# VectorE subtracts the outputs' low part from the PSUM bank in place of a second ScalarE copy and a GpSimd subtraction

## The reference, cut to what matters

```python
x = x + xattn(layernorm(x), ctx)     # out @ Wo + bo + lora(out, o_down, o_up)
x = x + ffn(layernorm(x))            # bit_linear, depthwise conv, silu, bit_linear
# in the attention, per head:
s = einsum(q, k) * SCALE;  p = softmax(s);  o = einsum(p, v)
```

## Time and profile before

| | |
|---|---|
| median of 3 runs | 1537.39 us (1535.62 to 1537.73) |
| profiled execution | 1535.5 us |
| its span in the trace | 1533.5 us |
| granted TensorE clock, mean | 0.983 of full |

### The profile page before, as it was taken

How to read it: one execution, slowest core, us unless ns; L and a number is a source line. 1 busy time by engine, 2 the same in 40 slices (tenths; PEclk the granted TensorE clock), 3 DMA queues, 4 the chain that set the end, 5 groups by cost and what they waited for, 6 DMA issues and landing times.

```text
span 1533.5 us, 33070 instructions
## 1 busy us (share of the span) xinstructions
PE 1409.5 (92%) x10604; PEld 1159.5 (76%) x10650; DVE 1195.5 (78%) x3059; ACT 1182.3 (77%) x3909; POOL 668.1 (44%) x1058
## 2 busy tenths in 40 slices
PE   7899999999999999999999999999999999999762
PEld 4688778787777878777787878788787777878541
DVE  4363698787969878796887878688787878788888
ACT  3477787978878797887879788787978788797832
POOL 2354444445444444544544454444445444444420
PEclk9999999999999999999999999999999999999985
DMA  9210100000010100000010000001000000100000
GB/s 279 53 31 16 31 16 28 20 28 30 24 34 15 33 11 28 30 28 29 15 44 1 29 28 28 29 15 44 8 23 28 28 29 15 44 1 1 29 15 14
DMA packets 41144, 47.13 MB, mean 31 GB/s; under 512 B 3024, under 2 KB 35216, under 8 KB 41104
## 3 DMA queue, kind: packets, MB, share of 16 engines
q1 hardware_dynamic: 41104, 46.62, 10.1%
HBM read 36.13 MB, written 10.49 MB: 30 GB/s over the span
## 4 chain that ended last, share of the span: by engine, by line
PE 43%; DVE 30%; ACT 17%; issue 9%; DMA 1%; DVEq 0%; POOL 0%; SPq 0%; POOLq 0%; ACTq 0%
PE PS L500 10%; ACT SM L751 8%; PE PS L462 6%; PE PS L443 5%; PE PS L513 5%; PE PS L478 4%; PE PS L487 4%; PE PS L452 3%; PE PS L591 2%; DVE HP L1003 2%; DVE GBS L1062 2%; DVE MX L914 2%; DVE GBS L1086 2%; DVE HP L1009 2%; ACT QM L719 2%
## 5 line engine op out<-in xcount | busy, mean ns | idle before, releaser
L1238 POOL TENSOR_TENSOR SM<-SM,RC 128x496 f32<-128x496 f32 (+1 forms) x512 | 324.2, 654 | 738.6 <-DVE RC L908 738.6
L751 ACT ACTIVATE SM<-PS,MX 128x124 f32<-128x124 f32 x1024 | 359.9, 367 | 159.1 <-DVE SM L916 155.8
L500 PE MATMUL PS<-KT,QM 128*128 128x128 f32 x2048 | 278.1, 279 | 24.0 <-ACT SM L751 24.0
L500 PEld LDWEIGHTS PS<-KT,QM 128*128 128x128 f32 x2048 | 249.4, 192 | 38.6 <-ACT SM L751 38.1
L751 ACT ACTIVATION_READ_ACCUMULATOR SM<-PS,MX 128x1 f32 x1024 | 212.2, 207 | 0.0
L1269 POOL TENSOR_TENSOR OTl<-OF,OTh 128x256 fp32r<-128x256 f32 x256 | 204.1, 797 | 10.4 <-ACT OF L745 10.4
L487 PE MATMUL PS<-IDF,SM 128*128 128x128 f32 x1024 | 168.4, 287 | 16.6 <-POOL SM L1238 16.5
L743 ACT ACTIVATE OTh<-PS 128x256 fp32r<-128x256 f32 x256 | 100.4, 392 | 93.5 <-PE PS L478 92.5
L914 DVE TENSOR_REDUCE MX<-PS 128x4 f32<-128x496 f32 x256 | 170.5, 666 | 0.4 <-issue 0.4
L478 PEld LDWEIGHTS PS<-PT,V 128*64 128x64 f32 x2048 | 106.6, 136 | 82.3 <-issue 75.4
L478 PE MATMUL PS<-PT,V 128*64 128x128 f32 x2048 | 168.6, 286 | 0.0
(11 more groups left out here) (166 smaller groups left out, 3511.5 us busy)
## 6 DMA issues: line engine op xcount, KB each, us to landing
XIN<-in_x SPq DMA_DIRECT2D x16, 512.0 KB, 3.5
XRES<-in_x SPq DMA_DIRECT2D x16, 512.0 KB, 4.6
out_y<-HP SPq DMA_DIRECT2D x15, 512.0 KB, 3.2
CRAW<-in_ctxT SPq DMA_DIRECT2D x16, 256.0 KB, 2.7
RRAW<-in_ctxT SPq DMA_DIRECT2D x32, 128.0 KB, 2.9
QM<-in_Wq SPq DMA_DIRECT2D x1, 1024.0 KB, 9.1
GBS<-in_Wo SPq DMA_DIRECT2D x1, 1024.0 KB, 14.0
k_ipa_columns<-HP SPq DMA_DIRECT2D x1, 1024.0 KB, 6.5
```

The lines of the kernel that those rows point to most:

```text
L500: m = mm(psS[:, h, :], QM[:, 2 * q + h // 2, h % 2, TOK * b:TOK * b + TOK], KT[:, 2 * q + h // 2, b, :], start=True, stop=True)
L751: m = act.activation(SM[s % 2][:, h, 0:ORG], psS[:, h, 0:ORG], ACT.Exp, bias=MX[s % 2][:, h:h + 1], accum_out=SU[s % 2][:, h:h + 1])
L1238: m = pool.tensor_tensor(part, part, RC[c % 2][:, 4 * i:4 * i + 4].unsqueeze(2).broadcast_to(shape), ALU.mult)
```

## The change

ScalarE copies the bank `psO` once, into `OTh`, and signals `ot_high` with that. VectorE gets a new function, `output_low`: it waits for `ot_high` and writes `OTl` = `psO` - `OTh`, reading the bank itself, and signals `ot_done`. It stands in VectorE's step behind `attend_sums` and V's copy and ahead of `attend_maxima`; in the drain it follows the order of `output_copies`. `p_v` waits for `ot_done` in place of `ot_high`, since VectorE now reads the bank after ScalarE. The tile `OF` and GpSimd's `attend_low` are gone.

```diff
@@ -186,7 +186,6 @@
         SM = [sb(f"SM{i}", [P, 4, TOK]) for i in range(2)]
         PT = sb("PT", [P, 4, TOK])
         OT = [[sb(f"OT{i}{c}", [P, 2, TOK], F32R) for c in range(2)] for i in "hl"]
-        OF = sb("OF", [P, 2, TOK])
         MX = [sb(f"MX{i}", [P, 8]) for i in range(2)]
         SU = [sb(f"SU{i}", [P, 8]) for i in range(2)]
         RC = [sb(f"RC{i}", [P, 8]) for i in range(2)]
@@ -467,7 +466,7 @@
                 if gc.exists():
                     q, b = divmod(c, NB)
                     pe.wait_ge(pt_done, gc.count(CHUNKS, c + 1))
-                    need(pe, ot_high, gc.count(CHUNKS, c))
+                    need(pe, ot_done, gc.count(CHUNKS, c))
                     if b == 0:
                         u = 2 + 6 * q
                         pe.wait_ge(unit_free[0], gc.count(UNITS // 2, (u + U_V[0]) // 2 + 1))
@@ -535,7 +534,7 @@
                         pe.wait_ge(unit_free[0], g.count(UNITS // 2, UNITS // 2))
                         pe.wait_ge(s_used, g.count(CHUNKS, CHUNKS))
                         pe.wait_ge(pt_done, g.count(CHUNKS, CHUNKS))
-                        pe.wait_ge(ot_high, g.count(CHUNKS, CHUNKS))
+                        pe.wait_ge(ot_done, g.count(CHUNKS, CHUNKS))
                         pe.wait_ge(fin_done, g.count(2, 0))
                     if j >= len(F1_BANKS):
                         pe.wait_ge(g_done, g.count(CT, j + 1 - len(F1_BANKS)))
@@ -740,9 +739,7 @@
                 gc, c = chunk_at(g, s - 3)
                 if gc.exists():
                     act.wait_ge(o_full, gc.count(CHUNKS, c + 1))
-                    act.activation(OT[0][c % 2][:], psO, ACT.Identity)
-                    need(act, ot_done, gc.count(CHUNKS, c))
-                    act.activation(OF[:], psO, ACT.Identity).then_inc(ot_high, 1)
+                    act.activation(OT[0][c % 2][:], psO, ACT.Identity).then_inc(ot_high, 1)
 
             def exponentials(g, s):
                 if g.exists():
@@ -906,6 +903,12 @@
                     dve.tensor_reduce(SU[c % 2][:, 4:8], SM[c % 2][:, :, ORG:TOK], AX.X, ALU.add).then_inc(sum_done, 1)
                     dve.wait_ge(sum_done, gc.count(CHUNKS, c + 1))
                     dve.reciprocal(RC[c % 2][:], SU[c % 2][:]).then_inc(rec_done, 1)
+
+            def output_low(g, s):
+                gc, c = chunk_at(g, s - 3)
+                if gc.exists():
+                    dve.wait_ge(ot_high, gc.count(CHUNKS, c + 1))
+                    dve.tensor_tensor(OT[1][c % 2][:], psO, OT[0][c % 2][:].bitcast(F32), ALU.subtract).then_inc(ot_done, 1)
 
             def attend_maxima(g, s):
                 if g.exists():
@@ -1181,6 +1184,10 @@
                     value_copy(g, n + HALVES)
                 if g.shift(1).exists(1):
                     value_copy(g.shift(1), n)
+                if is_drain(g) and n == 3:
+                    output_low(g, 2)
+                if n % 2 == 0 and not (is_drain(g) and n == 4):
+                    output_low(g, n // 2)
                 if n % 2 == 0:
                     attend_maxima(g, n // 2)
                 if g.reg is None and g.off == 0:
@@ -1261,14 +1268,6 @@
             for n in range(EARLY_HALVES, HALVES):
                 project(At(0), n)
 
-            def attend_low(g, n):
-                s, half = divmod(n, 2)
-                gc, c = chunk_at(g, s - 3)
-                if half == 1 and gc.exists():
-                    pool.wait_ge(ot_high, gc.count(CHUNKS, c + 1))
-                    pool.tensor_tensor(OT[1][c % 2][:], OF[:], OT[0][c % 2][:].bitcast(F32),
-                                       ALU.subtract).then_inc(ot_done, 1)
-
             def residual(g, n):
                 if n in (16, 18, 20, 22) and g.exists():
                     b = (n - 16) // 2
@@ -1286,7 +1285,6 @@
                     finish(g.shift(-1), n)
                 residual(g, n)
                 attend(g, n)
-                attend_low(g, n)
 
             run_groups(pool, steps)
```

## The result

The changed kernel takes **1543.0 us** in the median (1542.3 to 1544.5, six runs), the kernel before 1536.8 beside it (1535.5 to 1537.7): a ratio of 1.0043, interval 1.0030 to 1.0056. It is slower by 6.2 us, 0.4%. The direction was forecast, and the range held the time; the forecast itself, 13 us, was double.

What follows compares the result with a forecast made beforehand. No engine alone bounds the kernel; TensorE's few waits in 14 periodic groups decide. Terms 0.33 + 0.13 - 0.10 + 0.26 + 0.33 = +0.95 us a group, +13.3 in all, gave 1551 us (+0.9%), range 1536 to 1566.

Steps and rivals of the forecast that it cites:

- scores of step 7: TensorE's scores that wait for ScalarE's exponentials: VectorE's insertions in steps 4, 5 and 6 delay them by +0.33 us a group.
- lower bound: The forecast's faster end, 1546 us: each insertion taken at 0.34 less 0.08 us of overlap.
- Step 5: 0.33 - 0.33 = 0: VectorE in step 5: the insertion's 0.33 us is paid back by the tiny scale instruction no longer held by GpSimd's subtraction.
- a sign that the prediction had named as proving it wrong: Maxima of steps 6, 15 or 1 beginning no later than before; a group of 89 us or less was the alternative.
- steps 4 and 9: VectorE instructions held until GpSimd's normalisation ends (context's subtraction, convolution): the insertion fills that stall and costs 0.
- Step 7 itself: VectorE after V's copy in step 7: the subtraction makes the maxima start at 715.20 rather than 715.07, +0.13 us a group.
- the scores of step 2: They already wait on the exponentials of step 1, so that step's insertion costs its full +0.33 us a group.
- The scores of step 0: Insertions in steps 14 and 15 delay step 15's exponentials by 0.66 us; 0.40 of room leaves +0.26 a group.
- The scores of step 14: VectorE's delays in steps 10 and 11 against two copies fewer on ScalarE (-0.54): sum -0.10 us a group.
- Rival 1: No stall is filled: steps 4, 5 and 9 cost their 0.33 too, +1.0 us a group more, 1565 us; chance 0.17.
- Rival 3: VectorE's subtraction hides in waits for scores, ScalarE's release wins: -0.54 before step 14's scores, 1530 us; chance 0.12.
- Rival 2: GpSimd's freed port gives back more: step 10's gate also goes clear, +0.42 us a group, 1543 us; chance 0.13.

## Why the prediction was right in direction and double in size

- **The price** was near: the subtraction is 0.39 us long in the mean. At 703.18 it runs to 703.55 and the maxima start at 703.47: 0.08 of overlap, 0.29 of train. It is 0.29 in most steps, 0.32 in step 1 and 0.33 in steps 7 (718.05) and 11; the forecast took 0.33 for all. With these prices its own sum would have been +0.74 a group rather than +0.95, and its term for the scores of step 7 +0.25 rather than +0.33. "VectorE: DVE Perf Modes" of the Trainium skill, section "The DRAIN you can't avoid", has the next instruction wait until the pipe is empty, and adds that one which is not held starts earlier; these rows show the earlier start. The forecast's lower bound is added up wrong: with 0.26 in each place the terms are 0.19, 0.06, -0.24, 0.12 and 0.26, together +0.39 a group and 1543 us, not 1546, since the terms of steps 14 and 0 hold two insertions each. That this is the measured time is luck: its terms are not the measured ones.
- **Scores of step 7: the step that failed** is "Step 5: 0.33 - 0.33 = 0", which leaves out a second instruction that GpSimd held. VectorE's train from the sums of step 4 to the last of its maxima work in step 6 took 12.58 us before and 12.46 after (702.86 to 715.32). By steps, from sums to sums, step 4 changed by -0.09, step 5 by -0.33 and step 6 (to that last one) by +0.30; the forecast had 0, 0 and +0.33. The maxima work of step 6 so begins earlier in the group than before (19.03 us behind the scores of step 3, before 19.14), a sign that the prediction had named as proving it wrong; for steps 15 and 1 it did not come. The timeline of the kernel before:

```profile
699.55 0.16 DVE L906 TENSOR_REDUCE SU<-SM 128x4 f32<-128x16 f32 x1
...
706.63 1.19 POOL L1238 TENSOR_TENSOR SM<-SM,RC 128x496 f32<-128x496 f32 x2 [2.77 <-DVE RC L908]
...
707.28 0.40 DVE L865 TENSOR_SCALAR AM<-AR 128x4 f32<-128x4 f32 x1
...
708.59 1.14 DVE L1051 TENSOR_SCALAR GBS<-GBS,AS 128x256 f32<-128x256 f32 x4
...
712.13 0.16 DVE L916 TENSOR_TENSOR SM<-PS,MX 128x16 f32<-128x16 f32 x1
```

  Three insertions at 0.29 add 0.87, and the train is 0.12 shorter, so 0.99 came free. The context's subtraction gives 0.30 (0.99 to 0.69) and the scale 0.34 (it held up the next instruction from 708.05 to 708.59, now from 711.28 to 711.48); the forecast had these two. It didn't have the tiny maximum, 0.40 to 0.17: 0.23. The small rest is in the four normalisations of step 4 and the first of the maxima in step 5 (0.08 and 0.06). The maximum at 707.28 stood in the shadow of GpSimd's normalisation (its first part takes 1.01: 706.63 + 1.01 = 707.64) and ended at 707.68. In the changed kernel the subtraction stands between the reciprocal, which releases that normalisation, and the maximum, which so comes at 710.73, when the normalisation (to 710.87) is all but over. The insertion fills a stall, as the forecast said of steps 4 and 9; in step 5 there was one too, on an instruction whose rows were not looked up. Steps 4 to 6 alone confirm the sign; one GpSimd subtraction in step 5 confirms the scale's share. The maximum's share shows across the kernels: it takes 0.16 to 0.17 us in all ten that have the insertion in step 5, also in the two where GpSimd subtracts there, and 0.47 in the two experiments that keep the old path in step 5. So the insertion frees it, and not the missing subtraction. In the kernel with the new path in steps 11 to 13:

```profile
704.76 0.47 DVE L875 TENSOR_SCALAR AM<-AR 128x4 f32<-128x4 f32 x1
```

- The maximum and the scale read one input from SBUF, and were held by GpSimd all the same. "SBUF — State Buffer" of the Trainium skill, section "Who interferes with whom", counts `tensor_scalar`, which both are, among the operations that can take the port pair shared with GpSimd, when their operands meet conditions. The trace agrees, with 0.40 and 0.50 for 0.17.
- **Step 7 itself** (+0.13, measured +0.11) and **the scores of step 2** (+0.33, measured +0.33) held.
- **The scores of step 0** (+0.26, measured +0.29 and 0.06 at step 1) came out in the number, but only in part by the forecast's path. 0.16 of the 0.29 is TensorE's new wait for L1015, which stands on VectorE's train behind the insertion of step 14 and which the forecast did not have: from the scores of step 15 to P.V it is 4.63 us rather than 4.47. The kernel late in steps 1 and 15 keeps that wait (0.37) and those 0.16. The exponentials add only 0.13, and 0.06 at step 1. Steps 14, 15, 0 and 1 alone show the terms of steps 0 and 2 by themselves, the wait for the reduction with them (0.38).
- **The scores of step 14** were -0.10 and came to -0.20. ScalarE's release of 0.54 held (0.53 in the kernel with the dummy copy). What VectorE adds on that way was put 0.1 too high; with step 11 late it vanishes (-0.47 to -0.60).
- **The drain**: 0, and no more than 0.8 was found on the wait that was tried. The rest of what the profiled runs differ by, ahead of the first scores and behind the last, wasn't pursued.
- **The rivals.** Rival 1 (no stall is filled) fell: three are filled. Rival 3 names the right release, but VectorE isn't ahead of the scores at steps 15 and 1. Rival 2 gives 1543, the measured time, by a mechanism that did not occur: the gate of step 10 meets the residual addition as the forecast had it.

```profile
738.72 1.24 POOL L1275 TENSOR_TENSOR XRES<-XRES,BO 128x256 f32<-128x256 f32 x1
739.29 1.22 DVE L1012 SCALAR_TENSOR_TENSOR HP<-GBS,HP 128x512 f32<-128x512 f32 x1
```

  Its idea, that more stalls go than those counted, was right, in step 5.

## What to carry to other kernels

A change that moves work between engines in a periodic program is a sum of local prices, and here the parts measured alone added up: so it can be taken in the steps in which it pays (ScalarE binds, or an insertion on VectorE fills a stall) and left out where it costs (VectorE binds), 1526.7 us for 1543.0 in all steps. Before an insertion is priced at its duration, list every instruction behind it on its engine that lasts longer in some steps than in others, tiny ones too: the delay may move each out of another engine's shadow, as it did the maximum of step 5. A term that comes out right in the number can still hide a wait that nobody listed, as at the scores of step 0. And ask who reads the result: behind the maxima of step 1 the same instruction was free, because its reader stood ahead of a longer wait.

## What the hardware showed that was not expected

An instruction on 128x4 elements with a single SBUF input, 0.17 us by itself, took 0.38 to 0.62 us beside a GpSimd subtraction (0.62 in step 15 of the kernel with the new path in steps 4 to 6) and 0.40 to 0.47 beside a normalisation, ending within 0.04 us of that instruction's end. The new subtraction, with one input in PSUM and one in SBUF, ran beside GpSimd's normalisation (709.70 to 710.07, that one from 709.86) and kept its 0.37.
